# Second cross-attention rewritten: split single-pass matmuls, a second exponential in place in PSUM, and the chunk maxima first in each step

## The chip, the cores and the metric

One core of a Trainium2 chip. The metric is device time in microseconds (us) of one execution of the whole program. Before the change three runs took 6368.51, 6369.83 and 6371.42 us, median 6369.83 us.

## The reference, cut to what matters

Eight blocks are applied one after the other to x, 32 batches x 56 queries x 128 features: a cross-attention to a context of 1500 rows x 96 features and a feed-forward, four times. The change touches only the second cross-attention (L1), with 16 heads of width 64:

```
def _L1_xattn_ref(x, context, Wq, Wk, Wv, Wo, bo):
    q = (x @ Wq).reshape(B, Nq, h, dh)
    k = (context @ Wk).reshape(B, Nk, h, dh)
    v = (context @ Wv).reshape(B, Nk, h, dh)
    scores = jnp.einsum('bqhd,bkhd->bhqk', q, k) * scale
    attn = jax.nn.softmax(scores, axis=-1)
    out = jnp.einsum('bhqk,bkhd->bqhd', attn, v).reshape(B, Nq, h * dh)
    return out @ Wo + bo
```

with B = 32, Nq = 56, Nk = 1500, all in float32.

## The kernel before, in words

The key and value weights are folded into the queries and the output projection, so scores and sums are taken against the raw context. `attention` does this once per block and then runs `make_queries` and `attend_half` for each half of 16 batches. The two attentions of this form are L1 (second) and L3 (fourth); L3 takes other branches of the same function (`clip`, `values`) and stays as it is.

`attend_half` works on pairs of batches (8 pairs, NP, in a half). A pair is 24 steps k, 12 key tiles of 125 keys for each of its two batches. All 16 heads x 56 queries = 896 columns are done together, as two matmuls of 448 columns. In a step TensorE does, in this order:
- `weigh(i, k)` (L1218): 2 float32 matmuls, the exponentials of tile k times the context rows, added up in PSUM banks 4 and 5;
- `chunks` (L1105): 2 float32r matmuls of 500 columns for the *next* pair, a rough product of which only the maximum over the keys is wanted (the softmax shift); banks 6 and 7;
- `score(i, k + 2)` (L1197): 2 float32 matmuls, the shifted scores of the tile two steps ahead, into one of two buffers (banks 0-1, 2-3);
- an *aside* in steps 0, 4, 6, 12 and 17, which also uses banks 6 and 7: `turn_max` (L1111, a transpose of the maxima), `spread_den` (L1125, the reciprocal sums spread over partitions), `project` (L1133, the output projection). The next `chunks` waits until the aside's result has been read (`settled`).

ScalarE takes one exponential per step from PSUM into P (L1339) and copies the sums once per batch (L1321). VectorE takes the maxima of the chunks (`chunk_max`, L1354), turns them negative (L1371), inverts the sums (L1391) and normalizes (L1396, two instructions a batch). GpSimd casts the queries for the chunks (L1049), loads the float32r context (L1051) and the row of maxima (L1056). SP loads the float32 context twice per batch, by columns and by rows (L1010, L1014), and moves the sums (L1022, L1024). Semaphores alone set the order between the engines; within an engine the order is the one written out.

A half begins with the 24 chunks of its first pair ahead of any score. Its last pair has no chunks.

Of the kernel before, what the change touches and what calls it, by code (L numbers as in the profile page):

```python
# [13 lines left out]
F32 = mybir.dt.float32  # L14
F32R = mybir.dt.float32r
# [4 lines left out]
ALU = mybir.AluOpType  # L20
ACT = mybir.ActivationFunctionType
AX = mybir.AxisListType

B, NQ, D = 32, 56, 128
NK, DC = 1500, 96
T = B * NQ
CH = 448
NCH = T // CH
TT = 112
NT = T // TT  # L30
H = 16
HQ = H * NQ
HALF = HQ // 2
DH = 8
VW = 2 * (DH + 1)
KT, KP = 12, 125
KA = DC + 1
# [6 lines left out]
class Signal:  # L44
# [6 lines left out]
    def at(self, n):  # L51
        return self.base + n


class Core:
# [18 lines left out]
    def sb(self, name, shape, dt=F32, ctx=None):  # L74
        return (ctx or self.ctx).enter_context(self.nc.sbuf_tensor(name, shape, dt))
# [46 lines left out]
def v(core, name, p=128):  # L122
    n = VECS.index(name)
    return core.vec[0:p, n:n + 1]
# [96 lines left out]
def add_gated(core, src, gate):  # L221

    nc = core.nc
    with nc.Block() as block:
        @block.vector
        def _(dve):
            link = core.linker(dve, "dve")
            link(nc.vector.scalar_tensor_tensor(out=core.xT[:, :], in0=src[:, :],
                                                scalar=core.tg[:, gate:gate + 1], in1=core.xT[:, :],
                                                op0=ALU.mult, op1=ALU.add))  # L230
# [143 lines left out]
HB = B // 2  # L374
NP = HB // 2
# [1107 lines left out]
            S[name].base += n  # L1483


def uniform_if_nan(core, L, N, okays, csum, bo, ctx):


    nc, ps = core.nc, core.ps
# [1091 lines left out]
def build(nc, d, out):  # L2581
    with ExitStack() as ctx:
        core = Core(nc, ctx, d, out)
# [6 lines left out]
        with ExitStack() as c0:  # L2590
            qp = core.sb("L0_Qp", [D, T], F32, c0)
# [3 lines left out]
            with nc.Block() as block:  # L2595
                @block.vector
                def _(dve):
                    link = core.linker(dve, "dve")
                    link(nc.vector.tensor_tensor(core.OT[:, :], core.OT[:, :], qp[:, :], ALU.add))
# [8 lines left out]
        experts0(core, 1)  # L2608
        core.new_signals()
        layer_norm(core, core.xT, core.xn, "a1")  # L2610
        attention(core, "L1", core.xn, v(core, "L1_bo"), scale=0.125, dh=64)
        add_gated(core, core.OT, 2)
        core.new_signals()
        layer_norm(core, core.xT, core.xn, "f1")
# [145 lines left out]
```

## Time and profile before

| | us |
|---|---|
| median of 3 runs | 6369.83 |
| the profiled execution | 6366.63 |
| its span, first to last instruction | 6365.0 |
| PE, DVE, ACT, POOL busy | 4928.5, 2963.1, 2017.8, 369.5 |
| L1 attention, half 0 (1733.4 to 2514.4) | 781 |
| L1 attention, half 1 (2542.7 to 3322.1) | 779 |

"PE busy" is the union of matmul records; a record is longer than the time for which the array streams its columns, so matmul starts are what tells the pace.

### The profile page before, as it was taken

What the parts mean: (1) busy time and instruction counts of PE and PEld (TensorE: products, weight loads), DVE (VectorE), ACT (ScalarE), POOL (GpSimd) and SP (SyncE); (2) the same over time, 40 slices, a digit from 0 to 9 for tenths busy, and PEclk for the clock granted to TensorE, in tenths of its full rate; (3) what the DMA queues carried; (4) which work ended last, traced back from release to release, by engine and by line L of the source; (5) the groups of instructions that cost most, each with busy time, mean ns of one, the idle gap of its engine ahead of it and who ended that gap; (6) DMA issues with size and microseconds to landing.
All of it is one profiled execution on the core that took longest, in us unless ns stands there. A gap on an engine that the chain in (4) does not pass through costs nothing. (4 is left out here: it accounts for less than half of the span.)

```text
span 6365.0 us, 84062 instructions
## 1 busy us (share of the span) xinstructions
PE 4928.5 (77%) x31298; PEld 2880.9 (45%) x31298; DVE 2963.1 (47%) x3208; ACT 2017.8 (32%) x2291; POOL 369.5 (6%) x478
## 2 busy tenths in 40 slices
PE   7388886297399999899985222877578999889996
PEld 6266664276245554455542001555234555445553
DVE  6422224200343331433324766545436777577774
ACT  5266664011122222122221576322112222222222
POOL 0111110201200000000000000000000000000000
PEclk8699998555589999899997555888778999889997
DMA  4255552132111110111100400000001010000000
GB/s 122 61 126 115 122 125 60 60 118 82 44 32 44 33 41 12 48 35 43 33 15 14 112 4 1 0 1 0 12 4 37 23 30 26 19 25 27 30 22 10
DMA packets 89266, 281.13 MB, mean 44 GB/s; under 512 B 15938, under 2 KB 26125, under 8 KB 89008
## 3 DMA queue, kind: packets, MB, share of 16 engines
q1 hardware_dynamic: 71232, 235.66, 14.0%
q0 software_dynamic: 13312, 41.82, 2.5%
q10 hardware_dynamic: 4608, 2.10, 0.1%
q8 instruction: 75, 1.23, 0.1%
q14 instruction: 39, 0.32, 0.0%
HBM read 195.91 MB, written 7.86 MB: 32 GB/s over the span
## 5 line engine op out<-in xcount | busy, mean ns | idle before, releaser
L1354 DVE TENSOR_REDUCE L_mp<-ps 112x2 f32<-112x1000 f32 x768 | 916.7, 1199 | 928.0 <-PE ps L1105 920.9
L1197 PE MATMUL ps<-L_qp,L_ct 98*125 (+1 forms) x3072 | 1319.7, 552 | 8.8 <-DMA L_qp<-L_mt 8.8
L1105 PE MATMUL ps<-L_cr,L_qb 97*112 97x500 f32 x1536 | 672.3, 524 | 150.4 <-DVE L_mp L1354 59.4
L1197 PEld LDWEIGHTS ps<-L_qp,L_ct 98*125 98x125 f32 x3072 | 582.1, 191 | 404.3 <-issue 332.4
L1339 ACT ACTIVATE L_p<-L_p 125x896 f32<-125x896 f32 x384 | 365.0, 951 | 1062.4 <-DVE L_p L1385 1061.5
L1339 ACT ACTIVATE L_p<-ps 125x896 f32<-125x896 f32 x384 | 352.2, 917 | 1078.1 <-PE ps L1197 1078.1
L1218 PE MATMUL ps<-L_p,L_cn 125*97 125x448 f32 x1536 | 648.3, 544 | 0.0
L1385 DVE SCALAR_TENSOR_TENSOR L_p<-ps,L_lb 125x896 f32<-125x896 f32 x384 | 418.9, 1091 | 189.6 <-PE ps L1197 187.1
L1105 PEld LDWEIGHTS ps<-L_cr,L_qb 97*112 97x112 f32 x1536 | 256.2, 191 | 416.4 <-issue 237.3
L870 ACT ACTIVATE L_p<-ps,rk 125x896 f32<-125x896 f32 x384 | 384.9, 1008 | 81.0 <-PE ps L752 78.7
L1218 PEld LDWEIGHTS ps<-L_p,L_cn 125*97 125x97 f32 x1536 | 243.7, 164 | 315.2 <-issue 286.4
L769 PE MATMUL ps<-L_p,L_vs 125*32 125x112 f32 x6144 | 237.2, 274 | 83.8 <-ACT L_p L870 74.4
L752 PE MATMUL ps<-L_qs,L_ks 128*128 (+1 forms) x3072 | 239.1, 221 | 0.0
L1212 PE MATMUL ps<-L_p,L_values 125*32 125x112 f32 x6144 | 230.0, 268 | 8.6 <-ACT L_p L1339 8.6
L1212 PEld LDWEIGHTS ps<-L_p,L_values 125*32 125x32 f32 x6144 | 136.4, 110 | 174.0 <-issue 98.6
L769 PEld LDWEIGHTS ps<-L_p,L_vs 125*32 125x32 f32 x6144 | 140.4, 112 | 148.5 <-ACT L_p L870 98.1
L2404 ACT ACTIVATE batatt_kt<-ps,vec,bit_out 128x1500 f32<-128x1500 f32 x64 | 102.5, 1601 | 330.6 <-PE ps L2338 330.6
L752 PEld LDWEIGHTS ps<-L_qs,L_ks 128*128 128x128 bf16 x3072 | 172.8, 101 | 75.4 <-issue 57.4
L901 DVE COPY L_vs<-ps 125x432 f32<-125x432 f32 x128 | 77.2, 603 | 259.6 <-PE ps L741 258.0
L894 DVE TENSOR_TENSOR L_k_rest<-ps,L_k_part 128x500 f32<-128x500 f32 x96 | 65.1, 679 | 284.6 <-ACT L_k_part L837 284.6
L1049 POOL CAST L_qb<-L_qp 97x896 fp32r (+1 forms) x64 | 59.8, 934 | 2134.8 <-PE ps L1105 1919.2
L2433 DVE SCALAR_TENSOR_TENSOR batatt_kv<-ps,bit_out,batatt_brow 125x1536 f32<-125x1536 f32 x64 | 116.3, 1817 | 102.0 <-PE ps L2347 102.0
(419 smaller groups left out, 6129.4 us busy)
## 6 DMA issues: line engine op xcount, KB each, us to landing
L_ks<-L_k_part SPq DMA_DIRECT2D x192, 375.0 KB, 7.5
L_ct<-in_ctxT SPq DMA_DIRECT2D x64, 574.2 KB
L_cr<-in_ctxT POOLq DMA_DIRECT2D x64, 568.4 KB, 7.0
moe_w<-in_L_w SPq DMA_DIRECT2D x64, 512.0 KB
L_cn<-in_ctxN SPq DMA_DIRECT2D x32, 568.4 KB
cs_ct<-in_ctxT SPq DMA_DIRECT2D x32, 562.5 KB, 4.2
L_ct<-in_ctxT SPq DMA_DIRECT2D x32, 562.5 KB, 4.5
img_y<-in_ctxT SPq DMA_DIRECT2D x32, 562.5 KB, 4.6
```

Of the source, the lines that this page charges most:

```text
L752: mm = nc.tensor.matmul(SB[n % 2][:, m // 4, m % 4 * 2 * NQ:(m % 4 + 1) * 2 * NQ] .rearrange("p (j q) -> p j q", j=2), KS[s][:, m * NK + j ...
L769: mm = nc.tensor.matmul(ps[32 * g:32 * g + 32, 4, c:c + 2 * NQ], VS[s][:, j, m, :], P[:, n % 2, m * 2 * NQ:(m + 1) * 2 * NQ], start=(j == ...
L870: nc.scalar.activation(P[:, n % 2, :].rearrange("p (a n) -> p a n", a=2), SB[n % 2][0:KP], ACT.Exp, scale=rk[:, bass.ds(24 * i + n, 1)]).t ...
L1105: mm = nc.tensor.matmul(ps[0:TT, bank + a, 0:500], QB[s][:, t * TT:(t + 1) * TT], CR[s][:, c * 500:(c + 1) * 500], start=True, stop=True)
L1197: mm = nc.tensor.matmul(SB[n % 2][:, a, :], CT[s][0:KS, j * KP:(j + 1) * KP], query(i, s, a, KS), start=True, stop=True)
L1212: mm = nc.tensor.matmul(U[32 * g:32 * g + 32, c:c + 2 * NQ], VS[s][:, j, m, :], P[:, n % 2, m * 2 * NQ:(m + 1) * 2 * NQ], start=(j == 0 an ...
L1218: mm = nc.tensor.matmul(U[:, a, :], CN[s][:, j, :], P[:, n % 2, a * HALF:(a + 1) * HALF], start=(j == 0), stop=(j == KT - 1))
L1339: nc.scalar.activation(two(P[:, n % 2, :]), src, ACT.Exp, scale=sc).then_inc(S["exped"].sem, 1)
L1354: nc.vector.tensor_reduce(mp[:, 2 * k:2 * k + 2], ps[0:TT, bank:bank + 2, 0:500], AX.X, ALU.max).then_inc(S["chunk_maxed"].sem, 1)
L1385: nc.vector.scalar_tensor_tensor(out=two(P[:, n % 2, :]), in0=SB[n % 2], scalar=0.0, in1=two(LB[n // KT][:, :]), op0=ALU.min, op1=ALU.max) ...
L2404: nc.scalar.activation(KTs[:, s, :].rearrange("p (a m) -> p a m", a=3), ps[:, 3:6, 0:500], ACT.Identity, scale=sc, bias=v(core, which)).th ...
L2433: nc.vector.scalar_tensor_tensor(out=KV[p][:, s, :, :], in0=ps[0:KP, 3:6, :].rearrange("p b (t n) -> p (b t) n", n=D), scalar=sc[0:KP, :], ...
```

## The change

`attention(core, "L1", ...)` becomes `attention_wide(...)`, which calls a new `attend_wide` in the place of `attend_half`. What it does:

- *Three passes.* Each float32 operand is split into a float32r part and a float32r rest. One score matmul becomes high x high, high x rest, rest x high; so does one weigh matmul. TensorE gets 12 float32r matmuls of 448 columns in a step for the 4 float32 ones.
- *The splits.* GpSimd loads context columns and rows a second time, cast to float32r by the DMA, and subtracts them from raw copies that SP loads into one shared tile RAW; the same for the queries. Per batch: one cast (96x896), three subtractions (96x1500, 96x896, 125x1164), two casting loads and two raw loads.
- *The exponentials.* ScalarE takes the exponential twice: into PH, rounded to float32r, and then in place in the PSUM buffer of the scores, in float32. VectorE subtracts one from the other into PL (`rest`).
- *The order.* A step of TensorE is now chunks, weigh_hi (4 matmuls, needs PH), weigh_lo of the tile before (2 matmuls, needs PL), the aside, score of tile k+2 (6 matmuls; needs `rest(k)`, since the exponential now lives in the same buffer). The asides are in steps 0, 5, 7, 12 and 18.

```
+def attend_wide(core, tag, S, qp, N, bo, half, ctx):
...
+            def score(i, n):
+                s, j = n // KT, n % KT
+                if j == 0:
+                    pe.wait_ge(*at(f"keys_split{s}", 3 * i + 3))
+                    pe.wait_ge(*at(f"max_in{s}", 16 * i + 16))
+                pe.wait_ge(*at("p_split", 24 * i + n + 1))
+                k = slice(j * KP, (j + 1) * KP)
+                for a in range(2):
+                    q = slice(a * HALF, (a + 1) * HALF)
+                    nc.tensor.matmul(SB[n % 2][:, a, :], CH[s][:, k], QH[s][:, q], start=True, stop=False)
+                    nc.tensor.matmul(SB[n % 2][:, a, :], CH[s][0:DC, k], QL[s][:, q], start=False, stop=False)
+                    mm = nc.tensor.matmul(SB[n % 2][:, a, :], CL[s][:, k], QH[s][0:DC, q],
+                                          start=False, stop=True)
+                mm.then_inc(S["scored"].sem, 1)
+            def weigh_hi(i, n):
...
+                pe.wait_ge(*at("exped_hi", 24 * i + n + 1))
+                for a in range(2):
+                    p = PH[:, n % 2, a * HALF:(a + 1) * HALF]
+                    nc.tensor.matmul(U[:, a, :], NH[s][:, j, :], p, start=(j == 0), stop=False)
+                    mm = nc.tensor.matmul(U[:, a, :], NL[s][:, j, :], p, start=False, stop=False)
+            def weigh_lo(i, n):
+                pe.wait_ge(*at("p_split", 24 * i + n + 3))
+                for a in range(2):
+                    mm = nc.tensor.matmul(U[:, a, :], NH[s][:, j, :], PL[:, n % 2, a * HALF:(a + 1) * HALF],
+                                          start=False, stop=(j == KT - 1))
+                mm.then_inc(S["weighed"].sem, 1)
...
+            def aside(i, k, prev, nxt):
+                if k not in ASIDE:
+                    return
+                if nxt:
+                    pe.wait_ge(*at("chunk_maxed", 24 * i + 24 + k + 1))
...
+            def body(i, prev, nxt, after):
+                for k in range(24):
+                    if nxt:
+                        if k:
+                            settled(i, k - 1, prev, nxt)
+                        chunks(i + 1, k // 12, k % 12)
+                    if k % KT:
+                        weigh_hi(i, k)
+                        weigh_lo(i, k - 1)
+                        aside(i, k, prev, nxt)
+                    if k + 2 < 24:
+                        score(i, k + 2)
+                    elif nxt:
+                        score(i + 1, k - 22)
+                    if k % KT == 0:
+                        aside(i, k, prev, nxt)
+                        weigh_hi(i, k)
+                    if k % KT == KT - 1:
+                        weigh_lo(i, k)
...
+        @block.scalar
+                    act.wait_ge(*at("scored", 24 * i + n + 1))
+                    act.wait_ge(*at("weighed", 24 * i + n + 1))
+                    nc.scalar.activation(two(PH[:, n % 2, :]), SB[n % 2], ACT.Exp
+                                         ).then_inc(S["exped_hi"].sem, 1)
+                    nc.scalar.activation(SB[n % 2], SB[n % 2], ACT.Exp).then_inc(S["exped"].sem, 1)
...
+        @block.vector
+            def rest(i, n):
+                dve.wait_ge(*at("exped", 24 * i + n + 1))
+                dve.wait_ge(*at("weighed", 24 * i + n + 1))
+                nc.vector.tensor_tensor(two(PL[:, n % 2, :]), SB[n % 2], two(PH[:, n % 2, :].bitcast(F32)),
+                                        ALU.subtract).then_inc(S["p_split"].sem, 1)
+            def body(i, prev, nxt, after):
+                for k in range(24):
+                    if nxt:
+                        chunk_max(i + 1, k // 12, k % 12)
+                    if k + 1 < 24:
+                        rest(i, k + 1)
...
+        @block.gpsimd
+            def split_keys(i, s):
+                pool.dma_start(CH[s][0:DC, :], batch(d["ctxT"][:, 0:DC, :], i, s)
+                               ).then_inc(S[f"hi_in{s}"].sem, 16)
+                nc.gpsimd.tensor_copy(QH[s][0:DC, :], folded(i, s)).then_inc(S[f"keys_split{s}"].sem, 1)
...
+                nc.gpsimd.tensor_tensor(CL[s][:, :], RAW[0:DC, :], CH[s][0:DC, :].bitcast(F32),
+                                        ALU.subtract).then_inc(S[f"keys_split{s}"].sem, 1)
+                nc.gpsimd.tensor_tensor(QL[s][:, :], folded(i, s), QH[s][0:DC, :].bitcast(F32),
+                                        ALU.subtract).then_inc(S[f"keys_split{s}"].sem, 1)
...
-        attention(core, "L1", core.xn, v(core, "L1_bo"), scale=0.125, dh=64)
+        attention_wide(core, "L1", core.xn, v(core, "L1_bo"), 0.125)
```

`scored`, `exped_hi`, `exped`, `p_split` and `weighed` count the tiles of a half; `weighed` and `p_split` start at 2. So `weighed >= n + 1` on ScalarE means that `weigh_lo(n - 2)` is done, and `p_split >= n + 1` in `score(n)` that `rest(n - 2)` is. In the first pair of a half, GpSimd also fills a row of ones in each CH tile, and the row of maxima is moved only after both batches have been split.

## Rows read from the trace of the kernel before

**Rows 1.** Busy time, clock and DMA of each engine in one pair's stretch of L1.
```profile
core 0: us, PE busy (x) PEld busy (x) DVE busy (x) ACT busy (x) POOL busy (x), PEclk, DMA share, GB/s
1964.00:2055.00 91.00, 91.00 (x283) 46.34 (x282) 33.47 (x34) 24.12 (x27) 3.86 (x6) 1.00 0.13 38
```
**Rows 2.** Timeline of ACT: the copy of the sums in two successive pairs.
```profile
1917.45 0.92 ACT L1321 ACTIVATE L_ue<-ps 97x896 f32<-97x896 f32 x1 [0.68 <-PE ps L1218]
...
2008.58 0.92 ACT L1321 ACTIVATE L_ue<-ps 97x896 f32<-97x896 f32 x1 [0.68 <-PE ps L1218]
```
**Rows 3.** Timeline of one step: start, duration, engine, line, idle before and releaser.
```profile
2019.35 1.67 PE L1197 MATMUL ps<-L_qp,L_ct 98*125 x4
2019.55 1.20 DVE L1354 TENSOR_REDUCE L_mp<-ps 112x2 f32<-112x1000 f32 x1 [2.26 <-PE ps L1105]
...
2020.85 1.67 PE L1218 MATMUL ps<-L_p,L_cn 125*97 125x448 f32 x4
2021.05 0.92 ACT L1339 ACTIVATE L_p<-ps 125x896 f32<-125x896 f32 x1 [2.54 <-PE ps L1197]
...
2022.81 1.67 PE L1197 MATMUL ps<-L_qp,L_ct 98*125 x4
```
**Rows 4.** Groups by line: form, count | busy, mean ns | idle before, releaser.
```profile
L870 ACT ACTIVATE L_p<-ps,rk 125x896 f32<-125x896 f32 x384 | 384.9, 1008 | 81.0 <-PE ps L752 78.7
L1339 ACT ACTIVATE L_p<-ps 125x896 f32<-125x896 f32 x384 | 352.2, 917 | 1078.1 <-PE ps L1197 1078.1
L1385 DVE SCALAR_TENSOR_TENSOR L_p<-ps,L_lb 125x896 f32<-125x896 f32 x384 | 418.9, 1091 | 189.6 <-PE ps L1197 187.1
L1396 DVE TENSOR_TENSOR L_un<-L_ue,ps 97x448 f32<-97x448 f32 x64 | 36.9, 618 | 113.7 <-PE ps L1125 113.7
L713 POOL TENSOR_TENSOR L_k_part<-L_k_rest,L_k_part 128x500 bf16<-128x500 f32 x96 | 108.9, 1135 | 636.2 <-ACT L_k_part L842 636.2
L1197 PEld LDWEIGHTS ps<-L_qp,L_ct 98*125 98x125 f32 x3072 | 582.1, 191 | 404.3 <-issue 332.4
```
**Rows 5.** Timeline: hand-overs ACT to ACT, ACT to DVE, DVE to PE.
```profile
608.85 1.91 ACT L870 ACTIVATE L_p<-ps,rk 125x896 f32<-125x896 f32 x2
...
600.92 0.59 ACT L837 ACTIVATE L_k_part<-ps 128x500 bf16<-128x500 f32 x1 [2.14 <-DMA L_ks<-L_k_part]
601.54 0.68 DVE L894 TENSOR_TENSOR L_k_rest<-ps,L_k_part 128x500 f32<-128x500 f32 x1 [2.45 <-ACT L_k_part L837]
...
1788.60 1.20 DVE L1354 TENSOR_REDUCE L_mp<-ps 112x2 f32<-112x1000 f32 x1 [11.80 <-PE ps L1105]
1789.86 0.09 PEld L1111 LDWEIGHTS ps<-ident,L_mc 112*8 112x8 f32 x1 [0.51 <-DVE L_mp L1354]
```
**Rows 6.** Timeline of the asides and of a half's first scores; DMA issues to landing.
```profile
2031.33 1.74 PE L1125 MATMUL ps<-L_rc,ones 1*97 1x448 f32 x4
2708.29 3.82 PE L1133 MATMUL ps<-L_un,L_N 97*128 97x112 f32 x32
...
1780.94 5.66 PE L1197 MATMUL ps<-L_qp,L_ct 98*125 98x448 f32 x8 [4.51 <-DMA L_qp<-L_mt]
...
L_cr<-in_ctxT POOLq DMA_DIRECT2D x64, 568.4 KB, 7.0
L_ct<-in_ctxT SPq DMA_DIRECT2D x32, 562.5 KB, 4.5
L_qp<-L_mt POOLq DMA_DIRECT2D x64, 3.5 KB, 2.9
```
**Rows 7.** Clock beside PE's idle time, in short stretches of two other attentions.
```profile
5030.00:5033.00 3.00, 0.49 (x1) 0.45 (x2) 2.85 (x4) 0.00 (x0) 0.00 (x0) 0.81 0.00 0
...
654.00:657.00 3.00, 2.10 (x56) 1.44 (x48) 0.91 (x2) 3.00 (x6) 2.21 (x2) 1.00 0.63 174
...
5204.48 3.19 PE L1197 MATMUL ps<-L_qp,L_ct 98*125 x4
5207.47 0.82 PE L1157 MATMUL ps<-L_un,L_woe 128*128 128x112 f32 x3
```

More of the change, by code:

```diff
@@ L1483, in attend_half @@
             S[name].base += n
+WIDE = {"raw_in0": 16 * NP, "raw_in1": 16 * NP, "hi_in0": 16 * NP, "hi_in1": 16 * NP,
+        "keys_split0": 3 * NP, "keys_split1": 3 * NP, "cn_raw_in0": 16 * NP, "cn_raw_in1": 16 * NP,
+        "cn_hi_in0": 16 * NP, "cn_hi_in1": 16 * NP, "cn_split0": NP, "cn_split1": NP,
+        "qb_ready0": NP, "qb_ready1": NP, "ctr_in0": 16 * NP, "ctr_in1": 16 * NP,
+        "chunk_scored": 24 * NP, "chunk_maxed": 24 * NP, "max_ready": 2 * NP, "max_turned": 2 * NP,
+        "max_negated": 2 * NP, "max_in0": 16 * NP, "max_in1": 16 * NP,
+        "scored": 24 * NP, "exped_hi": 24 * NP, "exped": 24 * NP, "p_split": 24 * NP + 2,
+        "weighed_hi": 24 * NP, "weighed": 24 * NP + 2, "u_copied": 2 * NP + 1,
+        "den_out": 32 * NP, "den_in": 32 * NP, "den_inverted": 2 * NP, "den_spread": 2 * NP,
+        "u_normed": 2 * NP + 1, "projected": NP, "out_copied": NP}
@@ new lines, in attention_wide @@
+def attention_wide(core, L, src, bo, scale):
+    outer = ExitStack()
+    N = core.sb(f"{L}_N", [KA, H, D], F32, outer)
+    M = core.sb(f"{L}_M", [D, H, KA], F32, outer)
+    cq = core.sb(f"{L}_cq", [KA, H], F32, outer)
+    S = {n: core.sig(f"{L}_{n}") for n in [*WIDE, "ones_set"]}
+    with outer:
+        fold_weights(core, L, M, N, cq, scale, True, 64, None)
+        for half in range(2):
+            with ExitStack() as ctx:
+                qp = core.sb(f"{L}_qp{half}", [DC + 8, HB, HQ], F32, ctx)
+                make_queries(core, qp, M, cq, src, scale, half)
+                attend_wide(core, f"{L}{half}", S, qp, N, bo, half, ctx)
```

270 lines of the change are left out of this document (added).

## The prediction

> **What bounds the kernel now.** I read the page first (the table above: TensorE is busy for 4928 of 6365 us), then the busy time by stretches, to see the second attention alone. In the stretch of one pair TensorE is busy for all of 91.00 us at the full clock, 2.4 GHz, VectorE for 33.47, ScalarE for 24.12, GpSimd for 3.86 [rows 1]. So here every other engine waits for TensorE. The timeline gives the period: the same copy of the sums comes 91.13 us later one pair on [rows 2]. Inside a pair the timeline shows the step: scores start at 2019.35 and again at 2022.81, 3.46 us later; the four score records (8 passes, a float32 matmul being two records of two passes) stream in 2020.85 - 2019.35 = 1.50 us, 0.188 us a pass, and so do the weighing ones; the two float32r chunk matmuls get the other 0.46 us [rows 3]. 24 x 3.46 = 83.0, so the asides of a pair cost 8.1 us. The exponential starts 0.20 us after the scores have streamed, the chunk's maximum 0.20 us after the chunk [rows 3].
>
> **Passes.** 12 single passes replace 16: TensorE's own step falls to 12 x 0.188 + 0.46 = 2.72 us. If nothing else grew, that is 0.74 us off each of 384 steps, 284 us. No row shows a float32r matmul of 448 columns, but the chunks are float32r of 500 and take 0.23 each with their hand-overs [rows 3]; ends 0.188 and 0.23 x 448/500 = 0.206, and I take the pass of the rows, 0.188.
>
> **The new loop.** What the step lost is slack. Before, the next scores only needed the exponential. Now score(k+2) needs rest(k), rest(k) the second exponential, that the first, and the first waits for weigh_lo(k-2), which TensorE does in step k-1. Follow it from one weigh_lo to the second next:
> - last weighing matmul to ScalarE 0.20 [rows 3];
> - two exponentials. One is 0.917; in the timeline two of 1.008 follow each other in 1.91 together, so a second one adds 0.09 less than its length [rows 4, 5]. That is 0.92 + 0.83 = 1.75. The in-place write to PSUM has no row. By the slowest exponential of this size, 1.008, it adds 0.92; at the low end, 0.75, another tenth below.
> - ScalarE to VectorE 0.03: 600.92 + 0.59 = 601.51, start 601.54 [rows 5];
> - the subtraction: no row of 896 columns with two tensors, but 448 take 0.618 and a three-operand form of 896 takes 1.091 [rows 4]. I take 1.09, ends 1.00 and 1.15;
> - VectorE to TensorE's weight load 0.06: 1788.60 + 1.20 = 1789.80, load at 1789.86 [rows 5], and 0.15 before the matmul streams, between the 0.09 of a small load [rows 5] and the 0.19 of a load of 125 columns [rows 4];
> - on TensorE, 6 score passes 1.13, the chunks of the next step 0.46, weigh_hi 0.75, weigh_lo 0.38.
>
> Sum 0.20 + 1.75 + 0.03 + 1.09 + 0.21 + 1.13 + 0.46 + 0.75 + 0.38 = 6.00 us for two steps, 3.00 a step. It is longer than TensorE's 2.72, so the loop sets the pace and TensorE idles 0.3 a step, as one wait of about 0.6 in every second. VectorE's 1.20 + 1.09 = 2.29 and ScalarE's 1.75 a step stay below 3.00, but VectorE is no longer idle when an aside wants it. Steps: 24 x 3.00 = 72.0 for 83.0.
>
> On the second exponential the Trainium skill speaks too ("ScalarE: Activation LUTs", step by step, the profile stage): it calls PSUM the lower-latency destination for ScalarE. No row has an activation that writes PSUM. By the page the 0.83 would be an upper end; by the rows alone it is the middle.
>
> **The asides.** They now stand between weigh_lo and score, and need the maximum of the chunk of their own step. The chunk comes first in the step: from its end 0.20 to VectorE, 1.20 of maximum, 0.06 and 0.15 to TensorE, against the 1.13 us of weigh_hi and weigh_lo: at least 0.5 us of wait. Where VectorE still does rest(k) first it is up to 0.5 + 1.09 + 0.2 = 1.8. Before, the chunk lay ahead of 1.50 us of scores and this wait was 0 to 0.1. After spread_den the next chunks wait for the normalization, 0.20 + 2 x 0.618 + 0.2 = 1.6 us against 1.13 us of score: 0.5, and up to 1.3 behind a rest; before, 1.50 of weighing covered it. Also the score itself comes late, and with it the loop. So:
> - spread_den, twice a pair: own 1.50 (four records, as the scores) + 1.2 + 0.9 = 3.6, together 7.2. Its records are in [rows 6];
> - project: own 3.6 (32 records; the 3.82 of its row includes the last one's end [rows 6]) + 1.8 = 5.4;
> - turn_max, twice: the chunks of the step behind it wait until VectorE has negated the turned maxima, which is queued behind rest(k+1) and so behind two exponentials: about 1.6 each, 3.2.
>
> 15.8 for 8.1. A pair is 72.0 + 15.8 = 87.8 against 91.1: 3.3 us less. There are 7 such pairs in a half: 14 x 3.3 = 46 us.
>
> **The last pair of each half** has no chunks. The loop loses their 0.46: 5.54, 2.77 a step, where before 16 passes took 3.0. 24 x 0.23 = 5.5, twice 11 us.
>
> **The start of each half.** The first score needs both batches split, since max_row(0, 0) is queued on GpSimd behind both splits and two more casts. A subtraction on GpSimd takes 1.135 for 500 columns [rows 4], 2.27 ns a column: 3.4 for the 1500 key columns, 2.0 for the 896 queries, 2.6 for the 1164 row columns. The loads land 4.5 to 7.0 us after issue singly [rows 6]; the first batch's cast load is the fifth in GpSimd's queue, and I give it 19 us from the start. Then 19 + 5.4 (keys, queries) + 5 (raw rows) + 2.6 + 4.5 (raw keys) + 5.4 + 5 + 2.6 = 49.5, two casts and issues 2.9, the row of maxima 2.9 and its issue 0.5: 56. Before it was 1780.9 - 1733.4 = 47.5 [rows 6]. So +9 a half (3 with subtractions at the cast's pace, 14 with slow loads), +18 in all. In the steady pairs the same work has room: from score 12 to the need for the new keys lie 12 steps, 36 us, for 7.0 + 0.9 + 5.4 = 13 us; raw rows and keys 10 more. The sums' two small DMAs have 2 steps each. SP's invert is queued behind raw_rows and can be 1 or 2 us late, within the 1.2 and 0.9 above. No cover is left if subtractions take three times as long.
>
> **Sum.** -46 - 11 + 18 = -39. The profiled execution took 6366.6 (3.2 below the median shown), so 6327.6 there, and 6331 as a median.
>
> **The rivals.**
> - *The loop is longer than its 6.00 us* and the gain is gone: slower. The mechanism is the second exponential, in place in PSUM, on the path between every score and the next but one. Each 0.1 us of it costs 384 x 0.05 = 19 us. From an addition of 1.04 in the place of 0.83 on the change gains nothing; at 1.25 it is 41 us slower. 0.92, the end of the rows, with the weight load at 0.19 and the subtraction at 1.15 makes 6.19 and loses 36 of the 39. Against it: ScalarE's forms of this size differ by only a tenth [rows 4]. For it: nothing in the trace reads and writes one PSUM bank at a time, and each hand-over may be a tenth longer. At the end of this case I put +30, 6400.
> - *The loop is hidden* and TensorE's passes set the pace: 24 x 2.72 + 13 = 78.3, 12.8 less a pair, 14 x 12.8 = 179, with the last pairs -15 and the starts +18: 6194. For it: before, TensorE alone was busy [rows 1]. Against it: the waits are in the code, and the rows that fill them sum to more than 2 x 2.72.
> - *The clock falls.* In a stretch where TensorE was busy for 0.49 of 3.00 us the granted clock fell to a mean of 0.81, between 2.4 and 1.2 GHz, and at 1.2 GHz eight passes take 5207.47 - 5204.48 = 2.99 in the place of 1.50; a stretch with 2.10 of 3.00 us busy kept 2.4 GHz [rows 7]. At 1.2 GHz a step is 2 x 2.72 = 5.4; one step in ten like that adds 38 x 2.4 = 92 us: 6423. My longest idle time is 1.8 us. The Trainium skill ("TensorE: Matmul & The Clock Gate", a second failure mode) speaks for this rival: it says that idling a little between matmul groups, often enough, makes the clock go back and forth. [...]
> - *The change does not do what it says*: the splits are late in every pair and the scores wait at batch borders. Each us late costs 32; with 20 us of room I give it 2%, inside the slower cases.
>
> **How the numbers follow.** Forecast as worked out 0.50, its own range 6303 to 6357 (the pair's gain between 1.5 and 5.5). Between it and no change (the loop at the high end of the rows) 0.15. Longer loop, slower 0.21. Clock 0.05. Hidden loop 0.09. The range leaves out the hidden loop and the clock and reaches to the ends of the loop's terms on both sides: 6285 (subtraction 1.00 and second exponential 0.75, together -33, and starts of +3, another -12) to 6400. What this measurement can tell from no change is 0.2%, 12.7 us. Faster: 0.50 + 0.09 + 0.02 = 0.61; within it 0.13; slower 0.26.
>
> **What would show it.** Score starts of one pair alternate about 2.7 and 3.3, mean 3.0; every second score on TensorE is released by VectorE's subtraction, and the first exponential by the weighing; if TensorE has no idle time in plain steps, the loop was hidden. The second exponential's length decides the first rival. Copies of the sums one pair on are 87.8 apart. Spread_den and project wait for the chunk's maximum, 0.5 to 1.8 us. The first score of a half comes 56 us after its start. Granted clock 1.00 in the pairs. The forecast is wrong if the pair's period is outside 85.5 to 90.

## The result and the profile after

| | before | changed |
|---|---|---|
| median, us | 6370.62 (4 runs) | 6451.63 (4 runs, 6446.38 to 6454.08) |
| the profiled execution, and its span | 6366.63, 6365.0 | 6454.08, 6452.5 |
| mean period of a pair (twelve pairs) | 91.2 | 95.6 |
| first score after a half's start, half 0 and half 1 | 47.5, 46.6 | 65.7, 63.9 |

The ratio is 1.0126, with a 95% interval from 1.0108 to 1.0143: the change makes the kernel 1.3% slower. Forecast was 6331, 0.6% faster, and the time lies outside the range too.

The copies of the sums one pair apart, which answer to [rows 2], and the pair's stretch, which answers to [rows 1] (same columns):

```profile
2042.56 0.92 ACT L1840 ACTIVATE L_ue<-ps 97x896 f32<-97x896 f32 x1 [0.29 <-PE ps L1758]
...
2137.73 0.92 ACT L1840 ACTIVATE L_ue<-ps 97x896 f32<-97x896 f32 x1 [0.29 <-PE ps L1758]
```
```profile
2137.70:2230.70 93.00, 85.79 (x380) 64.87 (x378) 58.29 (x59) 43.32 (x52) 23.77 (x19) 0.94 0.26 62
```
This pair took 95.17; over the twelve pairs behind the first of each half the mean is 95.6. TensorE is no longer busy all the time (85.79 of 93.00, where [rows 1] had 91.00 of 91.00), and its granted clock is 0.94 in the place of 1.00. VectorE and ScalarE work about 1.8 times as long as before and GpSimd six times as long (23.77 for 3.86); none is full.

The groups of the new instructions, from the page (count | busy us, mean ns | idle before, releaser), beside [rows 4]:

```profile
L1888 DVE TENSOR_TENSOR L_pl<-ps,L_ph 125x896 fp32r<-125x896 f32 x384 | 419.1, 1091 | 522.7 <-ACT ps L1855 520.8
L1853 ACT ACTIVATE L_ph<-ps 125x896 fp32r<-125x896 f32 x384 | 352.1, 917 | 866.1 <-PE ps L1758 730.9
L1734 PE MATMUL ps<-L_qh,L_ch 97*125 97x448 f32 x768 | 317.3, 413 | 95.6 <-DMA L_qh<-L_qp 49.0
L1855 ACT ACTIVATE ps<-ps 125x896 f32<-125x896 f32 x384 | 350.4, 912 | 0.0
```
The exponential in place in PSUM takes 912 ns, no more than the one to SBUF (917), and the subtraction 1091. Two plain steps in the timeline, thinned out, which answer to [rows 3]:

```profile
2314.58 0.58 PE L1758 MATMUL ps<-L_pl,L_nh 125*97 125x448 f32 x2
2314.99 0.36 PE L1734 MATMUL ps<-L_qh,L_ch 97*125 97x448 f32 x1
2315.20 0.37 PE L1735 MATMUL ps<-L_ql,L_ch 96*125 96x448 f32 x1
2315.25 0.92 ACT L1853 ACTIVATE L_ph<-ps 125x896 fp32r<-125x896 f32 x1 [2.55 <-PE ps L1758]
2315.40 0.36 PE L1736 MATMUL ps<-L_qh,L_cl 96*125 96x448 f32 x1
...
2316.07 0.91 ACT L1855 ACTIVATE ps<-ps 125x896 f32<-125x896 f32 x1
...
2317.01 1.09 DVE L1888 TENSOR_TENSOR L_pl<-ps,L_ph 125x896 fp32r<-125x896 f32 x1 [1.85 <-ACT ps L1855]
...
2318.16 0.47 PE L1734 MATMUL ps<-L_qh,L_ch 97*125 97x448 f32 x1
...
2319.47 0.61 PE L1699 MATMUL ps<-L_cr,L_qb 96*112 96x500 f32 x2
...
2319.92 0.37 PE L1749 MATMUL ps<-L_ph,L_nh 125*97 125x448 f32 x1
```
A float32r pass of 448 columns comes 0.205 us after the one ahead (2314.99, 2315.20, 2315.40), not 0.188. The score at 2318.16 starts 0.06 after the subtraction ends (2317.01 + 1.09): here TensorE has waited for the loop. Starts of the exponential alternate about 2.90 (TensorE's own 12 x 0.205 + 0.46 = 2.92) and 3.25, some 6.16 for the two steps, 3.08 a step. So 24 plain steps take 73.9 and the asides of a pair the other 21.7.

An aside in the timeline:

```profile
2158.81 1.09 DVE L1888 TENSOR_TENSOR L_pl<-ps,L_ph 125x896 fp32r<-125x896 f32 x1 [1.61 <-ACT ps L1855]
2159.29 0.57 PE L1758 MATMUL ps<-L_pl,L_nh 125*97 125x448 f32 x2
2159.82 1.19 DVE L1870 TENSOR_REDUCE L_mp<-ps 112x2 f32<-112x1000 f32 x1
...
2161.14 1.74 PE L1711 MATMUL ps<-L_un,ones 1*97 1x448 f32 x4 [1.27 <-DVE L_mp L1870]
...
2163.94 0.58 PE L1735 MATMUL ps<-L_ql,L_ch 96*125 96x448 f32 x1
2164.31 0.58 PE L1736 MATMUL ps<-L_qh,L_cl 96*125 96x448 f32 x1
```
The chunk's maximum stands on VectorE behind the subtraction, and that behind two exponentials; the spread of the denominators waits for it, TensorE idles 1.27 us, and behind the spread the passes are 0.37 us apart: TensorE is at 1.2 GHz (the granted clock of 2164.00 to 2166.00 is 0.50).

The start of a half on GpSimd (idle time ahead of each and what ended it), and the first score:

```profile
1754.73 3.36 POOL L1631 TENSOR_TENSOR L_cl<-L_raw,L_ch 96x1500 fp32r<-96x1500 f32 x1 [10.88 <-DMA L_ch<-in_ctxT]
1758.06 2.08 POOL L1633 TENSOR_TENSOR L_ql<-L_qp,L_qh 96x896 fp32r<-96x896 f32 x1
1767.81 2.65 POOL L1643 TENSOR_TENSOR L_nl<-L_raw,L_nh 125x1164 fp32r<-125x1164 f32 x1 [7.67 <-DMA L_raw<-in_ctxN]
...
1777.20 3.34 POOL L1631 TENSOR_TENSOR L_cl<-L_raw,L_ch 96x1500 fp32r<-96x1500 f32 x1 [5.34 <-DMA L_ch<-in_ctxT]
1780.50 2.06 POOL L1633 TENSOR_TENSOR L_ql<-L_qp,L_qh 96x896 fp32r<-96x896 f32 x1
1789.26 2.63 POOL L1643 TENSOR_TENSOR L_nl<-L_raw,L_nh 125x1164 fp32r<-125x1164 f32 x1 [6.70 <-DMA L_raw<-in_ctxN]
...
1794.59 0.52 POOL L1649 DMA_DIRECT2D L_qh<-L_qp  x1
```
```profile
1801.34 0.71 PE L1734 MATMUL ps<-L_qh,L_ch 97*125 97x448 f32 x1 [25.76 <-DMA L_qh<-L_qp]
```
The span grew by 87.5. The twelve pairs between the first and the last of each half took 4.5 more each (+54) and the starts 18 and 17 more (+35). The first pair of a half took about as long as before, from its first score on. The last pairs took 2.6 less each (-5), and what lies outside this attention grew by some 4.

### The profile page after: what moved, and what is told of

Same layout as the page of the kernel before. It is cut to its first block and busy times, and to the rows that moved or that the text cites. A ratio compares the mean times of both kernels' runs of the same rounds, so it can differ in the third digit from the quotient of the medians.

```text
span 6452.5 us, 88818 instructions
## 1 busy us (share of the span) xinstructions
PE 4848.1 (75%) x32834; PEld 3176.4 (49%) x32834; DVE 3360.5 (52%) x3592; ACT 2324.0 (36%) x2675; POOL 697.6 (11%) x674
## 5 line engine op out<-in xcount | busy, mean ns | idle before, releaser
L1888 DVE TENSOR_TENSOR L_pl<-ps,L_ph 125x896 fp32r<-125x896 f32 x384 | 419.1, 1091 | 522.7 <-ACT ps L1855 520.8
L1197 PE MATMUL ps<-L_qp,L_ct 98*125 (+1 forms) x1536 | 672.4, 561 | 0.0
L1853 ACT ACTIVATE L_ph<-ps 125x896 fp32r<-125x896 f32 x384 | 352.1, 917 | 866.1 <-PE ps L1758 730.9
L1385 DVE SCALAR_TENSOR_TENSOR L_p<-ps,L_lb 125x896 f32<-125x896 f32 x384 | 418.7, 1091 | 187.0 <-PE ps L1197 184.5
L1734 PE MATMUL ps<-L_qh,L_ch 97*125 97x448 f32 x768 | 317.3, 413 | 95.6 <-DMA L_qh<-L_qp 49.0
L1105 PE MATMUL ps<-L_cr,L_qb 97*112 97x500 f32 x768 | 296.8, 473 | 118.4 <-DVE L_mp L1354 54.3
L1855 ACT ACTIVATE ps<-ps 125x896 f32<-125x896 f32 x384 | 350.4, 912 | 0.0
L1749 PE MATMUL ps<-L_ph,L_nh 125*97 125x448 f32 x768 | 298.2, 388 | 2.1 <-ACT L_ph L1853 2.1
L1750 PE MATMUL ps<-L_ph,L_nl 125*97 125x448 f32 x768 | 294.0, 383 | 0.0
L1735 PE MATMUL ps<-L_ql,L_ch 96*125 96x448 f32 x768 | 292.4, 381 | 0.0
L1736 PE MATMUL ps<-L_qh,L_cl 96*125 96x448 f32 x768 | 291.2, 379 | 0.0
```

Of the source, the lines that this page charges most:

```text
L1105: mm = nc.tensor.matmul(ps[0:TT, bank + a, 0:500], QB[s][:, t * TT:(t + 1) * TT], CR[s][:, c * 500:(c + 1) * 500], start=True, stop=True)
L1197: mm = nc.tensor.matmul(SB[n % 2][:, a, :], CT[s][0:KS, j * KP:(j + 1) * KP], query(i, s, a, KS), start=True, stop=True)
L1385: nc.vector.scalar_tensor_tensor(out=two(P[:, n % 2, :]), in0=SB[n % 2], scalar=0.0, in1=two(LB[n // KT][:, :]), op0=ALU.min, op1=ALU.max) ...
L1734: nc.tensor.matmul(SB[n % 2][:, a, :], CH[s][:, k], QH[s][:, q], start=True, stop=False)
L1749: nc.tensor.matmul(U[:, a, :], NH[s][:, j, :], p, start=(j == 0), stop=False)
L1853: nc.scalar.activation(two(PH[:, n % 2, :]), SB[n % 2], ACT.Exp).then_inc(S["exped_hi"].sem, 1)
```

## The experiments

Times are medians; the kernel before ran beside each group of them, at 6372.0, 6372.3, 6370.2 and 6368.5.

### 1. Chunks behind the weighing, aside behind the scores

```
                 for k in range(24):
+                    if k % KT:
+                        weigh_hi(i, k)
+                        weigh_lo(i, k - 1)
                     if nxt:
...
                         chunks(i + 1, k // 12, k % 12)
-                    if k % KT:
-                        weigh_hi(i, k)
-                        weigh_lo(i, k - 1)
-                        aside(i, k, prev, nxt)
...
+                    aside(i, k, prev, nxt)
                     if k % KT == 0:
-                        aside(i, k, prev, nxt)
                         weigh_hi(i, k)
```


> The changed kernel with the old order of a step back: weigh_hi, weigh_lo, then the chunks, the score, and the aside behind the score. Everything else of the change stays. Theory A (the order is at fault: the chunks' 0.46 us lie inside the loop through the exponentials, and the asides wait for the maximum of their own chunk): plain steps fall from a mean of 3.08 to TensorE's own 12 x 0.205 + 0.46 = 2.92, the asides lose 3 to 5 us a pair, together some 8 us in each of 14 pairs: about 6340, less than before's 6370. Rival B (the loop through the exponentials sets the pace whatever the order, the clock and the starts cost the rest): the steps stay at 3.0 to 3.1 and the time above 6420.

Measured: 6367.4 (10 runs), 0.9998 of before [0.9987, 1.0009], 84 us below the changed kernel. The plain steps are flat at 2.90, TensorE's own passes; a pair takes 88.6 in the first half. So the order alone takes back the whole loss, with the same instructions. In the second half a pair takes 91.0. One long step of 9.2 to 11.8 us remained in every pair but the first of each half, at its first spread.

### 2. Chunks first as in the change, only the asides behind the scores

```
                         weigh_lo(i, k - 1)
-                        aside(i, k, prev, nxt)
...
+                    aside(i, k, prev, nxt)
                     if k % KT == 0:
-                        aside(i, k, prev, nxt)
```


> Chunks first in each step as in the changed kernel, and only the asides (turn, spread, project) moved from before the step's scores to behind them. Chunks behind weighing plus asides behind scores together brought 84 us. Theory A, that both halves of that order count: the plain steps keep alternating 2.90 and 3.26 (mean 3.08), because the chunk still stands between the restart of the loop and the weighing, while the asides lose the part of their wait that the scores now cover, 2 to 3 us in a pair: 28 to 42 us in 14 pairs, so about 6415 (6400 to 6430). Rival B, the aside's place is all of it: 6370, and plain steps at 2.90. Rival C, only the chunk's place counts: 6440 to 6455.

Measured: 6453.9 (4 runs), 1.0130 [1.0115, 1.0146]: no change, rival C. The scores now cover the wait ahead of the spread, but it comes back behind it: TensorE idles 1.32 us up to 2159.14, ahead of the next chunks, for the normalization. So the 84 us of experiment 1 need the chunks' new place. Whether it gives them all by itself is open: the chunks were not moved with the asides left where they were.

### 3. TensorE's waits filled with matmuls of zero weights

```
+            def warm(k, n):
+                for _ in range(n):
+                    nc.tensor.matmul(U[:, 0, :], ZW[:, :], PH[:, k % 2, 0:HALF], start=False, stop=False)
```
In a pair 26 such matmuls run, at the places that the expectation names.

> The changed kernel with float32r matmuls of zero weights, added onto the open sums (they add nothing), in the places where TensorE waits beside the asides: four before the wait for the chunk's maximum in steps 5, 7 and 18, three or four before the chunks of steps 1, 6, 13 and 19. Theory A (the clock falls to 1.2 GHz because of these waits, and that is a large part of the loss): the granted clock in the pairs goes from 0.93-0.95 to above 0.98 and a pair gets 2.5 to 3 us shorter, 35 to 42 us in all: about 6412. Rival B (the cold stretches cost nothing, since the loop has slack, or the added matmuls cost as much as they save): within 10 us of 6452.

Measured: 6428.5 (4 runs), 1.0089 [1.0072, 1.0106]: 23 us less, between the two theories. Two stretches of pairs (columns as in [rows 1]), in the changed kernel and then with the waits filled:

```profile
1900.00:2400.00 500.00, 456.96 (x1959) 342.82 (x1958) 303.37 (x303) 224.88 (x265) 123.22 (x92) 0.92 0.26 61
2700.00:3250.00 550.00, 500.65 (x2154) 375.37 (x2153) 335.95 (x335) 248.77 (x292) 135.77 (x102) 0.93 0.26 62
...
1900.00:2400.00 500.00, 473.01 (x2139) 361.27 (x2140) 306.07 (x305) 226.94 (x268) 123.67 (x92) 0.96 0.25 61
2700.00:3250.00 550.00, 518.81 (x2400) 396.01 (x2399) 346.49 (x346) 258.59 (x304) 141.29 (x104) 0.99 0.26 63
```
In the second half, where the granted clock rose from 0.93 to 0.99, the mean pair fell from 95.7 to 92.9; in the first, 0.92 to 0.96, from 95.6 to 94.6. The 26 fillers take some 5.3 us a pair themselves, so the clock costs the changed kernel more than these 23 us, if fillers help in no other way; how much more, this experiment does not show.

### 4. The second exponential written to SBUF

```
-                    nc.scalar.activation(SB[n % 2], SB[n % 2], ACT.Exp).then_inc(S["exped"].sem, 1)
+                    act.wait_ge(*at("p_split", 24 * i + n + 1))
+                    nc.scalar.activation(two(EX[:, n % 2, :]), SB[n % 2], ACT.Exp).then_inc(S["exped"].sem, 1)
```
The scores then wait only for this exponential (`exped`), and the subtraction reads EX.

> The changed kernel with the second exponential written to a tile of its own in SBUF (two buffers) in the place of the scores' PSUM buffer, so that score(k+2) waits for the second exponential and no longer for VectorE's subtraction. Theory A (the loop of exponentials and subtraction sets the plain step): the loop loses about 1.15 us of its 6.2, TensorE's 2.92 takes over, steps fall from 3.08 to 2.92 and the waits for a subtraction at the head of a score go: 4 to 6 us a pair, 56 to 84 in all, 6370 to 6395. Rival B (VectorE's queue at the asides is the cost, not the loop): plain steps fall but the pair hardly does, above 6430. The second exponential itself: by the low end of the prediction an SBUF target costs 0.92, in PSUM it took 0.912.

Measured: 6553.3, 1.0278 [1.0261, 1.0296]: 102 us slower than the changed kernel. The exponential takes 912 ns there as well, so PSUM as its target was neither gain nor loss. What grew is the subtraction, now with two inputs in SBUF, wherever GpSimd works:

```profile
2204.95 1.09 DVE L1891 TENSOR_TENSOR L_pl<-L_ex,L_ph 125x896 fp32r<-125x896 f32 x1 [0.71 <-ACT L_ex L1858]
2206.52 3.43 POOL L1632 TENSOR_TENSOR L_cl<-L_raw,L_ch 96x1500 fp32r<-96x1500 f32 x1 [2.60 <-DMA L_ch<-in_ctxT]
2208.11 2.78 DVE L1891 TENSOR_TENSOR L_pl<-L_ex,L_ph 125x896 fp32r<-125x896 f32 x1 [0.76 <-ACT L_ex L1858]
2209.91 2.92 POOL L1634 TENSOR_TENSOR L_ql<-L_qp,L_qh 96x896 fp32r<-96x896 f32 x1
2211.93 1.86 DVE L1891 TENSOR_TENSOR L_pl<-L_ex,L_ph 125x896 fp32r<-125x896 f32 x1
```
Alone 1.09, beside GpSimd 2.78 and 1.86, and GpSimd's own goes from 2.08 to 2.92. The Trainium skill ("SBUF — State Buffer", Who interferes with whom) says that a VectorE instruction with two SBUF inputs contends with a GpSimd instruction that reads SBUF. The trace agrees: the two long subtractions end 0.94 and 0.96 us after GpSimd's instruction (2210.89 and 2209.95, 2213.79 and 2212.83), as if they had run only then. In the changed kernel, whose subtraction has one input in PSUM, it is 1.09 throughout. This experiment says nothing clean about the loop.

### 5. The row of maxima of batch 0 ahead of batch 1's splits

```
-            for s in range(2):
-                split_keys(0, s)
-                split_rows(0, s)
+            split_keys(0, 0)
+            split_rows(0, 0)
...
             max_row(0, 0)
+            split_keys(0, 1)
+            split_rows(0, 1)
```


> The changed kernel with one move at the start of each half: GpSimd moves the row of maxima of batch 0 before it splits batch 1, not after. Theory A (the serial splits behind one shared raw tile delay the first score, 65.8 us after the start against 47.5 before): the first score comes at about 47 us, 18 us earlier in each half, some 36 us in all: 6415. Rival B (the first scores then wait for batch 1 or for the row's DMA behind the loads): less than 15 us in all, with a wait of TensorE at step 10 of the first pair.

Measured: 6407.9 (4 runs), 1.0058 [1.0042, 1.0075]: 44 us less, and the first score comes 45.1 and 45.2 us after the start of its half, for 65.7 and 63.9. The queue on GpSimd was the price of the starts.

### 6. Experiments 1 and 5 together

> The order of the first experiment (weighing, chunks, scores, aside) with the row of maxima of batch 0 ahead of batch 1's splits. The two gains lie in different stretches (pairs, and the start of a half), so theory A, that the start is a chain of its own, expects 6367 - 40 = 6327 (6318 to 6340), below both kernels. Rival: with the pairs now bound by TensorE the splits of batch 1, which now come later, hold the first pair: 6345 to 6365.

Measured: 6342.0 (5 runs), 0.9950 [0.9937, 0.9964]. The starts gave 20 and 19 us, as in experiment 5; but the pairs took 90.6 and 91.8 on average in the place of 88.6 and 91.0, most of it in the steps of the two spreads, 12 us in the first half alone. Those steps were still unexplained.

### 7. The changed kernel without its second exponential

```
-                    nc.scalar.activation(SB[n % 2], SB[n % 2], ACT.Exp).then_inc(S["exped"].sem, 1)
...
-                dve.wait_ge(*at("exped", 24 * i + n + 1))
+                dve.wait_ge(*at("exped_hi", 24 * i + n + 1))
```
The kernel leaves out the remainder of the exponential, so its results are other numbers; its time is what is asked for.

> The changed kernel without the second exponential: ScalarE no longer overwrites the scores in PSUM, and the subtraction takes the plain scores and follows the first exponential (what is left out: the remainder of the exponential, so the low pass weighs other numbers). Theory A, that TensorE's own 2.92 us sets most steps and the loop of two steps adds only the 0.36 us of every second: plain steps fall to 2.90 flat, 0.16 x 24 = 4 us a pair, and some of the asides' waits go, 1 to 3 us a pair: 70 to 95 us in 14 pairs, about 6370 (6350 to 6390). Rival B, the three passes with the asides set the pair and the second exponential costs nothing: 6440 to 6455. Rival C, the second exponential is most of the pair: the pair falls under 85 us and the kernel under 6320.

Measured: 6434.9 (4 runs), 1.0091 [1.0076, 1.0107]: only 17 us less, though the plain steps did fall to 2.90 flat. The steps at the spreads grew: in the pair shown here the two at the first spread take 6.82 and 8.93 us, where the same pair of the changed kernel has 4.16 and 7.54. And TensorE's clock is lower: the granted clock over 1900 to 2400 is 0.90, for 0.92. The timeline of VectorE and of TensorE at the first spread:

```profile
2188.18 1.09 DVE L1887 TENSOR_TENSOR L_pl<-ps,L_ph 125x896 fp32r<-125x896 f32 x1 [0.69 <-ACT L_ph L1853]
2192.45 0.85 DVE L1892 RECIPROCAL L_qp<-L_qp 8x112 f32<-8x112 f32 x1 [3.17 <-DMA L_qp<-L_ue]
2193.33 1.20 DVE L1869 TENSOR_REDUCE L_mp<-ps 112x2 f32<-112x1000 f32 x1
...
2194.58 0.71 PE L1699 MATMUL ps<-L_cr,L_qb 96*112 96x500 f32 x2 [3.29 <-DVE L_mp L1869]
...
2196.90 3.29 PE L1711 MATMUL ps<-L_un,ones 1*97 1x448 f32 x4
```
The inversion of the denominators waits 3.17 us for their DMA, the next chunk's maximum waits behind it on VectorE, and TensorE for that. Where the DMA's time goes:

```profile
2180.94 0.27 SPq L1585 DMA_DIRECT2D L_raw<-in_ctxN  x1
2181.61 0.72 SPq L1592 DMA_DIRECT2D L_qp<-L_ue  x1
```
The copy of the sums had ended at 2177.09. SP held the small DMA until the 568 KB load ahead of it could go, and VectorE could go on at 2192.45, 10.8 us after the DMA's issue; two casting loads of GpSimd were issued beside it, at 2181.60 and 2182.12. This chain hardly depends on how fast the steps are: where VectorE waits at its end in the pairs, the issue comes 3.4 to 5.5 us after the copy and VectorE goes on 9.8 to 12.1 us after the issue, in the changed kernel and in experiments 1 and 7 alike. A faster kernel only waits longer. With experiment 1's order VectorE waits 2.54 us for it in the same way.

### 8. Experiment 6 with TensorE's waits filled

> As the kernel with both gains (weighing, chunks, scores, aside; early row of maxima), and matmuls with zero weights in TensorE's waits for VectorE around the asides, 4 or 3 of some 0.2 us each. Theory A, that what is left of the asides' price is partly the clock at 1.2 GHz behind waits of 1 to 2 us: another 15 to 25 us, the clock of the pairs from 0.95 to above 0.97, 6305 (6295 to 6318). Rival B, the added matmuls only stand in the way of the chunks and scores that end the waits: same as without them or up to 15 us above.

Measured: 6359.1 (11 runs), 0.9981 [0.9972, 0.9990]: 17 us slower than experiment 6, rival B and 2 us beyond it, although the clock over 2700 to 3250 rises from 0.92 to 0.97. Two groups of four fillers in a pair (steps 1 and 13) stand where there is no wait in this order and make steps of 2.90 into 3.71.

### 9. Experiment 6 with the denominators two steps later

```
-            ASIDE = (0, 5, 7, 12, 18)
+            ASIDE = (0, 7, 9, 12, 20)
...
-                    if k == 3 and prev:
+                    if k == 5 and prev:
                         invert(i - 1, 1)
...
-                    if k == 15:
+                    if k == 17:
                         invert(i, 0)
```
Norm, projection and output copy move with them.

> As the kernel with weighing, chunks, scores, aside and the early row of maxima (6342), but the inversion of the denominators on VectorE, their spread, the norm, the projection and the output copy each two steps later. Theory A, that in this order the inversion, which stands in VectorE's queue ahead of the next chunk's maximum, waits for the denominators' DMA (2.5 us at 2164.5) and that this is what leaves TensorE idle 1.8 us ahead of the spread and brings its clock down: the wait goes in both asides of a pair, with it 1.8 to 2.5 us each and the 1 to 2 us of slower passes behind, 5 to 8 us a pair, so 70 to 110 us less in 14 pairs: 6250 (6225 to 6275). Rival B, the asides' own passes and the norm set these steps: 6335 to 6350. Rival C, the clock falls at the asides with or without that wait, only the wait itself goes: 6290 to 6310.

Measured: 6228.7 (5 runs), 0.9781 [0.9768, 0.9795]: 113 us below experiment 6 and 2.2% faster than before. VectorE's waits for the denominators are gone, the granted clock in the twelve pairs is 0.98 for experiment 6's 0.92, and TensorE's waits in 500 us (1900 to 2400) are:

```profile
PE ps L1735 <- DVE L_pl L1888: 11.4, 19, 1.0
PE ps L1712 <- DVE L_mp L1870: 0.9, 6, 0.2
PE ps L1720 <- DVE L_mp L1870: 0.3, 2, 0.2
```
(us in all, times, longest). A pair takes 81.7 to 81.9, every one of them.

### 10. Experiment 7 with the denominators two steps later

> The changed kernel without the second exponential (left out: the remainder of the exponential, so the low pass weighs other numbers), with the inversion, spread, norm, projection and output copy two steps later. Without the second exponential alone the plain steps fell to 2.90 flat and the time only by 17 us, VectorE then waiting 2.8 us on average for the denominators. Theory A, the saved time was lost in that wait: 5 to 7 us a pair come back, 6435 - 85 = 6350 (6330 to 6370). Rival B, the wait for the denominators only took the place of another one: 6425 to 6440.

Measured: 6295.6 (4 runs), 0.9882 [0.9867, 0.9897]: 139 us less than experiment 7, more than theory A gave. The pairs fall from 95.0 to 85.0: 69.8 of plain steps and 15.2 of asides.

### 11. The changed kernel with the denominators two steps later

> The changed kernel with only the inversion, spread, norm, projection and output copy two steps later. In it VectorE waits for the denominators' DMA 5.3 us in 600 us, so theory A expects little: 6440 (6430 to 6455). Rival: 6400 or less, if the idle 1.0 to 1.3 us ahead of the spread comes from that wait after all.

Measured: 6431.1 (4 runs), 1.0090 [1.0075, 1.0106]: 20 us less than the changed kernel, so the late denominators were a small part of its loss. With experiment 10 it gives the price of the second exponential in this order, with that wait away from both: 6431 - 6296 = 135 us. Pairs take 94.0 on average against 85.0; 4.1 of the difference is in the plain steps (3.08 against 2.91) and 4.9 at the asides.

### 12. Experiment 9 without the second exponential

> The fastest kernel so far (6228.7: weighing, chunks, scores, aside; early row of maxima; denominators two steps later) without the second exponential (left out: the remainder of the exponential, so the low pass weighs other numbers). In the changed kernel's order, with the denominators later too, leaving it out brought 6431 - 6296 = 135 us. Theory A, it cost that only because the chunks stood between the loop's restart and its weighing; in this order every plain step is TensorE's own 2.9 us and the second exponential is hidden except where TensorE waits 0.5 to 0.7 us for the subtraction at the asides, about 2 us a pair: 6205 (6190 to 6230). Rival B, the second exponential has a price of its own on the path in any order: 6090 to 6150.

Measured: 6228.5 (4 runs), 0.9777 [0.9761, 0.9793]: the same as experiment 9. The 135 us are zero in this order. The two orders differ in the chunks' place and the asides' place, and the row of maxima is early here. The equality hides two terms. Seven pairs take 81.5 to 81.6, but five take 84.4 to 86.1: two steps at a spread are longer there (5.58 and 7.24 us in one), and the granted clock in the twelve pairs is 0.955 for 0.979. Against that the last pairs are 5 to 6 us shorter.

## Why the prediction was wrong

- **Passes, too short.** 0.188 was taken and 0.206 named as the other end; it is 0.205. TensorE's own step is 2.92, not 2.72. The loop's two steps are 6.16 for 6.00: passes and chunks 2.98 (2318.16 to the next score at 2321.14) for 2.72, the hand-over to ScalarE 0.26 for 0.20, the subtraction to the score 0.06 for 0.21. 24 steps take 73.9 for 72.0, 1.9 us a pair.
- **The second exponential and the subtraction, right.** 912 ns and 1091, starting 0.82 and 0.94 apart in the loop, 1.76 for the 1.78 forecast. The first rival's mechanism (a slow write to PSUM) did not happen.
- **The asides, the step that failed:** 15.8 forecast, 21.7 measured, 5.9 us a pair. Each aside was priced as its own work and waits, after which the steps go on at the loop's pace with the granted clock at 1.00. That last term, the clock, put at nothing, is what failed, as far as the trace lets the time be added up. It shows when a whole pair is added up from the trace (means of the twelve pairs, us):

| | forecast | changed kernel | experiment 9 |
|---|---|---|---|
| TensorE's work at 2.4 GHz | 71.9 | 78.6 (as in experiment 9) | 78.6 (with its shortest waits) |
| its waits | 15.9 | 10.6 | 1.5 |
| time lost to 1.2 GHz, at most | 0 | 6.4 | 1.7 |
| a pair | 87.8 | 95.6 | 81.8 |

  The forecast's work is 24 x 2.72 and 6.6 for the asides; its waits are 6.7 in the loop and 9.2 at the asides. In the changed kernel TensorE has no record running for 8.4 us of a pair; 2.2 more is what is left over, and I take it for waits too short to show between records. The loss to the clock is my estimate: the mean granted clock is 0.93, so TensorE is at 1.2 GHz for some 13 us of a pair, and at half the clock at most half of that is lost (a pass takes 0.37 there for 0.205). Against the forecast the work is 6.7 longer, mostly the passes, and the waits are 5.3 shorter, so these two together miss by 1.4; the clock adds up to 6.4. That is the 7.8 by which the pair was missed.
- **Why this order has such waits.** With the second exponential and the wait for the denominators both gone (experiment 10) the asides take 15.2. That this is near the 15.8 is chance, for the 15.8 was worked out with the second exponential in place. The other 6.5 us go in two parts, 4.9 with the second exponential (experiments 10 and 11) and 1.6 with the denominators (95.6 to 94.0 a pair, experiment 11), and in each part idle time and time at 1.2 GHz go together (the granted clock is 0.93, 0.94 and 0.96 in the changed kernel and experiments 11 and 10). Experiments 1 and 2 show that the order counts (84 us, with the chunks' place needed for it), experiment 12 that the second exponential costs nothing in sum in experiment 9's order. A reading of the timelines that no run proves: the working named the subtraction ahead of the chunk's maximum as a wait of TensorE, and left out that, with the chunks ahead of the weighing, this wait holds the weighing too, with it the next exponentials, and through them VectorE's next subtraction.
- **The denominators.** The forecast gave their two DMAs two steps each and SP a delay of 1 to 2 us. In the changed kernel's pairs SP issues the first of them 3.3 to 4.2 us after the copy of the sums, and VectorE's inversion starts 10.2 to 11.8 us after that issue; VectorE waits up to 1.5 us for it.
- **The clock, 0.05 forecast, present in every pair.** The trace of the kernel before had a sign of it that the forecast did not use, in a stretch of a feed-forward: one wait of 1.00 us, and TensorE is at 1.2 GHz behind it.

```profile
3400.03 1.62 PE L1964 MATMUL ps<-L1f_hh,L1f_wd 128*128 128x448 f32 x2 [1.00 <-DVE L1f_hh L2000]
...
3401.00:3402.00 1.00, 1.00 (x2) 0.38 (x2) 0.19 (x1) 0.00 (x0) 0.00 (x0) 0.50 0.00 0
```
  In the changed kernel the clock falls 26 times in 1900 to 2400 and 2700 to 3250. Of these falls 19 come behind a spread, with 0.4 to 1.3 us of idle time ahead of the spread, and six of the others behind waits of 1.1 to 2.1 us elsewhere. The Trainium skill ("TensorE: Matmul & The Clock Gate", A second HAM failure mode), which the prediction named as speaking for this rival, was the better guide: small idle times, clock back and forth. But experiment 9 has a fall behind a wait of only 0.16, at a spread, so the idle time may not be all of it. The clock's price lies between experiment 3's 23 us and my estimate of 12 x 6.4 = 77 us in the twelve pairs. Since TensorE would have waited for other engines in part of that time, the 77 is an upper end. Where between them it lies was not separated.
- **The starts**: +18 and +17 for +9 each. The first subtraction came at 19.1 for 19, and the six subtractions were as priced (3.4, 2.1, 2.6 each). The three loads that each wait for the one RAW tile took 7.7, 6.7 and 6.7 us for 5, 4.5 and 5 (+6.6), and the row of maxima 6.7 for 3.4 with its issue (+3.3), for it is issued behind two casting loads. Experiment 5 shows that the place in the queue was the price. Together some 17 us more than forecast.
- **The first pairs** of the halves were counted with the gain of the others, 3.3 us each, and gained nothing; **the last pairs** gained 5 us in all for the 11 forecast.

The twelve pairs are 7.8 us each above the forecast (94), the first pairs 7, the starts 17, the last pairs 6 and the rest outside this attention 4. That makes 128, and the forecast of -39 and the measured +87.5 are 126.5 apart. That the loop would be in sight and that the starts would cost was right; the sign of the pairs was not, since 5.9 us more at the asides and 1.9 in the steps outweigh a forecast gain of 3.3 a pair. The forecast called itself wrong if the pair's period is outside 85.5 to 90: it was 95.6.

So the passes saved are real. In an order in which TensorE has something to do while VectorE works, and with the denominators' chain given two more steps, the same instructions give 6228.7, 142 us below before. That is near the forecast's hidden loop (6194, with pairs of 78.3 at 0.188 a pass; they take 81.8), which the change does not reach in its own order.

## What to carry to other kernels

When work moves from a full engine to two others in a ring, look where in the step the engine restarts after its wait, and put first there what feeds the ring; work that only uses the time (here the chunks) goes behind it. Price an instruction that waits in an in-order queue by everything queued behind it, and a chain with a fixed length (a small DMA behind a large load) by its absolute time: after a speed-up it is the next wait, and a test of one change alone can show almost nothing (17 us for the second exponential with that wait in place, 135 without it). Do not price waits alone where TensorE is nearly full: look at the granted clock behind each wait in the trace at hand, and give the time at 1.2 GHz a term of its own. Where the gain is the small difference of large terms, the range must carry the error of each.

## What the runs showed of the hardware

- A float32r pass of 448 columns takes 0.205 us with its weight load at 2.4 GHz; the passes inside a float32 matmul of that size took 0.188 each [rows 3].
- ScalarE's exponential of 125x896 takes 912 ns in place in PSUM and 912 from PSUM to SBUF in float32.
- The clock can fall behind the spread (a matmul with one contraction row) with hardly a wait ahead of it. In experiment 9, windows of 1.5 and 1.0 us (columns as in [rows 1]) around the spread at 2090.47, which follows an idle time of 0.16 us:

```profile
2089.50:2091.00 1.50, 1.34 (x6) 0.72 (x6) 1.33 (x2) 0.97 (x2) 0.00 (x0) 1.00 0.00 0
2091.00:2092.00 1.00, 1.00 (x4) 0.24 (x2) 0.59 (x1) 0.00 (x0) 0.00 (x0) 1.00 0.00 0
2092.00:2093.00 1.00, 1.00 (x5) 0.69 (x5) 0.76 (x2) 0.00 (x0) 0.00 (x0) 0.82 0.00 0
2093.00:2094.00 1.00, 1.00 (x4) 0.82 (x3) 0.39 (x1) 0.00 (x0) 0.00 (x0) 0.50 0.00 0
2095.00:2096.00 1.00, 1.00 (x4) 0.90 (x3) 0.85 (x1) 1.00 (x2) 0.00 (x0) 0.50 0.00 0
2096.00:2097.00 1.00, 1.00 (x6) 0.84 (x5) 1.00 (x2) 0.10 (x1) 0.00 (x0) 0.97 0.00 0
```
  TensorE counts as busy all through but for that idle time, and is at 1.2 GHz from about 2092.6 to 2096.0. The same spread in the kernel before left the clock at 1.00 for the whole pair [rows 1]; what differs around it (float32 passes there, float32r here) was not tried apart, and so the cause stays open. Each of experiment 9's twelve pairs has one such fall, behind one of its spreads.
